# Loads of edge attributes and weights issued by ScalarE; SyncE fetches nine tiles of source rows in place of seven

## The chip, the cores and the metric

The kernel runs on one core of one Trainium2 chip. The metric is the device time of one execution in microseconds (us). A core has TensorE (PE, matmuls; PEld is its weight load), VectorE (DVE), ScalarE (ACT), GpSimd (POOL) and SyncE (SP), each with an instruction queue of its own; they wait for each other through semaphores. SP, ACT and POOL can issue DMAs.

## The reference

A graph layer over N = 6250 nodes of 128 channels and E = 106250 edges, sorted by their destination, followed by a residual sum and a layer norm:

```python
ef  = relu(edge_attr @ We1 + be1) @ We2 + be2          # edge_attr: E x 64
tw  = sigmoid(edge_weight[:, None] @ Wt + bt)          # E x 128
ef  = ef * tw
combined = concatenate([x[src], ef], axis=1)
msg = relu(combined @ Wn1 + bn1) @ Wn2 + bn2
out = segment_sum(msg, dst, N) + x
y   = layernorm(x + out)                               # N x 128
```

All of it is float32.

## The kernel before, in words

**The split of the work.** The first half of `Wn1` meets only `x[src]`, so the kernel first multiplies all nodes, adds `bn1`, and writes the product to DRAM as `node_table` (6250 rows of 512 B). An edge then needs its source's row of that table. `Wn2` is applied after the sum over edges. Edges go in groups of 512, a *pair* is two groups (1024 edges, 8 tiles of 128 edges), a *super* is two pairs (2048 edges). There are 104 pairs and 52 supers.

**One pair, as it runs through the engines.** PE transposes the edge attributes (`psT`, L839), ACT copies them out (`eaT`, L630), PE does the first edge layer (`psH`, L875), ACT its relu (`h<-psH`, L671), PE the second (`psE`, L887), and DVE multiplies it by the edge's weight factor `tw`, an ACT sigmoid (L663), into `efw` (L1162). PE multiplies `efw` by the second half of `Wn1` (`psM`, L862). DVE adds the gathered rows, `h<-psM,gathered` (L1141, function `pre`, semaphore `pre_ready`). ACT does the relu in place (`h<-h`, L596), and PE sums edges over their destinations by a product with one-hot tiles (`psS`, L820), which ACT copies out (`found`, L593) and DVE adds to the sums (L1105). Step s of the program works on all these stages at once, each for a pair further back: `psT`, `psH` and `tw` for pair s, `psE` and `efw` for pair s-1, `psM` and `pre` for pair s-2, `h<-h` and `psS` for pair s-3.

**The order on an engine is the order of the code.** Nothing is scheduled by a tool. Every four steps the loop body repeats (`BODY = 4`), and every four steps some blocks of finished nodes are put out (staging, two small PE products, the layer norm, a store by ACT at L694).

**Gathers.** POOL issues one indirect DMA for each tile of 128 edges (L536), 8 for each pair from pair 4 on, into one of four places of `gathered` (pair modulo 4). Before the gathers of pair p it waits until `pre` of pair p-4 has read that place.

**Rows fetched by SP.** Of some pairs the eighth tile isn't gathered by POOL. SP fetches its 128 rows one by one: it loads 8 node numbers from `src_rows` into registers (L496) and issues one DMA of one row for each (L501), into one of two buffers `row_tiles`; ACT copies the full buffer into `gathered` (`move_rows`, L655, semaphore `rows_moved`), and `pre` of that pair waits for it too. Before, these pairs are 20, 32, 44, ..., 92, so 7 tiles and 896 rows. Tile n+2 may only be fetched when tile n has been moved.

**Loads.** SP also issues the loads of edge attributes (`ea`, L442, 512 KB) and of edge weights (`ew`, L448, 1 MB written, each weight to all 128 partitions), one each for each super, into two buffers. A load of `ea` waits until the transposes of the super two back are done, a load of `ew` until the sigmoids of it are. The rows are paced by these loads: behind a load of `ea` 8 rows, behind a load of `ew` 8 or 16.

Of the kernel before, what the change touches and what calls it, by code (L numbers as in the profile page):

```python
# [40 lines left out]
DVE_ENGINE = mybir.EngineType.DVE  # L41
# [3 lines left out]
P = 128  # L45
TILES = 4
# [22 lines left out]

W1, IDS = W + 1, 13  # L70
ROW_TILE = PAIR * TILES - 1
ROW_LOAD, ROW_EVERY, ROW_FIRST, ROW_FROM = 8, 3, 5, 4


PART = (6, PAIR * TILES - 6)
# [2 lines left out]
def gnn_kernel(nc, x, src, dst, edge_attr, edge_weight, We1, be1, We2, be2, Wt, bt, Wn1, bn1, Wn2, bn2, out):  # L78
# [27 lines left out]
    with ExitStack() as ctx:  # L106
# [168 lines left out]

        def row_pair(n):

            return (ROW_FIRST + n * ROW_EVERY) * BODY

        def row_tile_of(p):  # L280

            turn = p // BODY - ROW_FIRST
            if p % BODY or turn < 0 or turn % ROW_EVERY or p >= PAIRS - 1:
                return None
            return turn // ROW_EVERY

        def row_tiles_by(turn):

            if isinstance(turn, int):
                return max(0, (turn - ROW_FIRST) // ROW_EVERY + 1)  # L290
            return turns["done"]

        def gathered_by(turn):

            if isinstance(turn, int):
                return turn * PART[1] - row_tiles_by(turn)
            return turns["done"] * (ROW_EVERY * PART[1] - 1) + (ROW_FIRST - ROW_EVERY + turns["of"]) * PART[1]

        def wait(eng, semaphore, value):

            if not (isinstance(value, int) and value <= 0):
                eng.wait_ge(semaphore, value)
# [124 lines left out]
        N_WEIGHTS = len(loads_act) + len(loads_sp)  # L427


        @block.sync  # L430
        def _(sp):
            def load_x(c):
                sp.dma_start(x_sb[:, c * XCH:(c + 1) * XCH, :],
                             x_blocks[:, c * XCH:(c + 1) * XCH, :]).then_inc(x_in[c], 16)

            def load_rows(tile, a, landed):
                last, first, second = by_group(a)
                for to, of in ((tile[0:SG, 0, :], last), (tile[SG:P, 0, :], first), (tile[0:ROWS[1], 1, :], second)):
                    sp.dma_start(to, of).then_inc(landed, 16)

            def load_edges(slot, start):
                sp.dma_start(ea[slot][:, :, :],  # L442
                             edge_attr[bass.ds(start, SE), :].rearrange("(g p j) f -> p g (j f)", p=P, j=TILES))\
                    .then_inc(ea_in[slot], 16)

            def load_weights_of(slot, start):

                sp.dma_start(ew[slot][:, :, :].rearrange("p g e -> p (g e)"),  # L448
                             edge_weight[bass.ds(start, SE)].rearrange("(a e) -> a e", a=1).to_broadcast([P, SE]))\
                    .then_inc(ew_in[slot], 16)  # L450

            def load_raw_e(n, a, b):

                part = src[E - SE:E] if a < SG else src[0:SE]
                sp.dma_start(raw_e[:, a:b, :], part.rearrange("(g p j) -> p g j", p=P, j=TILES)
                             [:, a % SG:(b - 1) % SG + 1, :]).then_inc(raw_e_in[n], 16)

            load_raw_e(0, 0, 2)
            for c in range(CHUNKS):
                load_x(c)  # L460
                if c == 1:
                    load_raw_e(1, 2, 4)
                if c == 3:
                    load_raw_e(2, 4, 8)
                    load_rows(src_rows, src, src_in)
            sp.dma_start(x_sb[0:LAST, FULL, 0:C], x_last).then_inc(x_in[CHUNKS], 16)
            load_rows(dst_rows, dst, dst_in)
            for to, of in loads_sp:
                sp.dma_start(to, of).then_inc(weights_in, 16)

            for b, (rows, n) in enumerate(BLOCKS):
                sp.wait_ge(table_ready, b + 1)
                sp.dma_start(table_blocks[:, b, :] if b < FULL else table_last,
                             table_sb[b][0:rows, 0:n * C]).then_inc(table_out[min(b // RING, 2)], 16)
                if b == RING:
                    load_edges(0, E - SE)
            load_weights_of(0, E - SE)
            sp.wait_ge(span_ready, 2)
            for r in range(2):
                sp.dma_start(spans_dram[r * P:r * P + ROWS[r], :], span_i[0:ROWS[r], r, :]).then_inc(span_out, 16)  # L480
            load_edges(1, 0)
            sp.wait_ge(span_out, 32)
            sp.dma_start(spans[:, :, :], spans_dram.rearrange("(a g) k -> a g k", a=1)).then_inc(spans_in, 16)
            for to, of in loads_late:
                sp.dma_start(to, of).then_inc(late_in, 16)
            load_weights_of(1, 0)

            def fetch_rows(n, first, last):

                p = row_pair(n)  # L490
                g = p * PAIR + ROW_TILE // TILES
                j = ORDER[ROW_TILE % TILES]
                if first == 0 and n >= 2:
                    sp.wait_ge(rows_moved, n - 1)
                for at in range(first, last, ROW_LOAD):
                    nodes = nc.values_load_multi_w_load_instructions(  # L496
                        src_rows[g % P:g % P + 1, g // P, at * TILES + j:(at + ROW_LOAD - 1) * TILES + j + 1:TILES],
                        engines=(mybir.EngineType.SP,), min_val=0, max_val=N - 1,
                        skip_runtime_bounds_check_because="an edge's source, which the inputs bound")[1]
                    for r, node in enumerate(nodes):  # L500
                        sp.dma_start(row_tiles[at + r:at + r + 1, n % 2, :], table[bass.ds(node, 1), :])\  # L501
                            .then_inc(rows_in[n % 2], 16)

            sp.wait_ge(src_in, 48)
            wait_table(sp)
            per = 2 * ROW_EVERY
            for m in range(2, SUPERS):
                n, part = (m - ROW_FROM) // per, (m - ROW_FROM) % per
                at = [P * x // ROW_LOAD // per * ROW_LOAD for x in (part, part + 1)]
                fetched = n >= 0 and row_tile_of(row_pair(n)) is not None  # L510
                sp.wait_ge(eaT_ps, (m - 1) * 2)
                load_edges(m % 2, (m - 1) * SE)
                if fetched:
                    fetch_rows(n, at[0], at[0] + ROW_LOAD)
                sp.wait_ge(tw_ready, (m - 1) * 2)
                load_weights_of(m % 2, (m - 1) * SE)
                if fetched:
                    fetch_rows(n, at[0] + ROW_LOAD, at[1])
            sp.wait_ge(last.y_done, 1)
            sp.dma_start(out_last, x_sb[0:LAST, FULL, 0:C]).then_inc(y_out, 16)  # L520

# [40 lines left out]
        def _(act):  # L562
# [48 lines left out]
            def step(i, k):  # L611
# [16 lines left out]
                if live(i, k, 0):  # L628
                    act.wait_ge(eaT_ps, s + 1)
                    nc.scalar.activation(eaT[:, k % 2, :], psT[:, :], ACT.Copy).then_inc(eaT_ready, 1)  # L630
                if s < RAW - RAW_BEFORE - 1:
                    copy_raw(s)
                if s == 0:
# [4 lines left out]
                if live(i, k, 0):  # L638
                    if s < BODY:
                        for n in ([], [0], [1], [2, 3])[s]:  # L640
                            weigh(n)
                    else:
                        weigh(s)
                    if s:
                        relu_h1(s)
                if s == RAW - RAW_BEFORE - 2:
                    copy_raw(s + 1)

# [343 lines left out]
        def _(dve):  # L992
# [174 lines left out]
            def pre(g, i, k):  # L1167
# [3 lines left out]
                if isinstance(g, int) and g < RAW // PAIR:  # L1171
                    rows = raw_pairs[g]
                    if g < RAW_BEFORE // PAIR:
                        dve.wait_ge(table_ready, len(BLOCKS) + (g + 1) * PAIR)
                    else:
                        dve.wait_ge(raw_ready, (g + 1) * PAIR - RAW_BEFORE)
                else:
                    rows = gathered[:, at, :]
                    turn = i - 1 if k < MSG_LAG else i
                    dve.wait_ge(gather_in[place][0], turn * (16 * PART[0]))  # L1180
                    if place == 0:
                        dve.wait_ge(gather_in[place][1], gathered_by(turn) * 16)
                        wait(dve, rows_moved, row_tiles_by(turn))
                    else:
                        dve.wait_ge(gather_in[place][1], turn * (16 * PART[1]))
                make_pre(h[:, at, :], psM[:, :, :], rows).then_inc(pre_ready, 1)
# [260 lines left out]
                    dve.wait_ge(last.shift_ready, 1)  # L1447
                    make_row(last, 0, 0)

            main_loop(dve, DVE_ENGINE, step, finish, end, ahead, ROW_FIRST, ROW_EVERY)  # L1450


# [23 lines left out]
```

## Time and profile before

| | us |
|---|---|
| median of 3 runs | 1438.06 (1436.29 to 1439.51) |
| the profiled execution, its own time | 1437.05 |
| its span in the trace | 1435.3 |
| POOL busy | 783.2 |
| PE busy (PE weight loads) | 966.9 (722.8) |
| DVE busy | 649.6 |
| ACT busy | 580.0 |

No engine is busy all the time, so the busy shares alone don't name a bound: the waits do. "Remote" as the releaser of a wait means that the profile doesn't name who ended it, and the end of a matmul is modelled in the trace. A "q" behind an engine's name marks what its sequencer does, such as the issue of a DMA.

### The profile page before, as it was taken

How to read it: one execution, taken by the hardware profiler on the slowest of the kernel's cores; microseconds unless marked ns; L12 is line 12 of the kernel's file. 1: busy time of each engine (PE TensorE's matmuls, PEld its weight loads, DVE VectorE, ACT ScalarE, POOL GpSimd, SP SyncE). 2: the span in 40 equal slices, each digit the busy share in tenths (PEclk: the TensorE clock that was granted, in tenths of full speed). 3: DMA queues.
4: the chain of work that ended last, by engine and by line, in shares of the span. 5: the costliest groups of instructions: out<-in, count | busy, mean ns of one | idle time of the engine just before them, and what ended most of it. 6: DMA issues, size and time to landing. Idle time of an engine off the chain costs nothing.

```text
span 1435.3 us, 18308 instructions
## 1 busy us (share of the span) xinstructions
PE 966.9 (67%) x5031; PEld 722.8 (50%) x5032; DVE 649.6 (45%) x1688; ACT 580.0 (40%) x656; POOL 783.2 (55%) x834
## 2 busy tenths in 40 slices
PE   3638767676677767666767667676766766765765
PEld 3626544554555545444545455555444545553454
DVE  1425533444445445344444444444543635544446
ACT  1316433443444425443444344443443534442442
POOL 7270456555655555556555565556555555655640
PEclk7768888798898889888878788889988977887978
DMA  6433332333423323333233233333332423333310
GB/s 183 142 110 110 103 114 89 95 114 93 131 83 108 114 88 115 106 100 124 85 91 121 92 101 113 100 121 89 105 114 85 136 86 112 112 102 112 96 30 18
DMA packets 72025, 148.62 MB, mean 104 GB/s; under 512 B 18295, under 2 KB 47030, under 8 KB 65254
## 3 DMA queue, kind: packets, MB, share of 16 engines
q1 hardware_dynamic: 42918, 89.72, 18.4%
q0 software_dynamic: 26400, 54.12, 14.3%
q10 hardware_dynamic: 2592, 3.48, 0.7%
q8 instruction: 45, 0.74, 0.2%
q14 instruction: 70, 0.57, 0.1%
HBM read 140.85 MB, written 6.40 MB: 103 GB/s over the span
## 4 chain that ended last, share of the span: by engine, by line
another core or an unknown queue 42%; ACT 21%; PE 19%; issue 11%; DVE 5%; ACTq 2%; DVEq 0%
ACT tw L663 9%; PE psS L820 6%; PE psM L862 5%; ACT h L596 4%; PE psH L875 4%; PE psE L887 2%; ACT h L671 2%; ACT eaT L630 1%; ACT found L593 1%; ACT x_sb L684 1%; DVE efw L1162 1%; DVE onehot L1147 1%; ACT staged_own L699 1%; DVE h L1141 1%
## 5 line engine op out<-in xcount | busy, mean ns | idle before, releaser
L536 POOL DMA_INDIRECT gathered<-node_table,src_e x793 | 751.6, 948 | 594.6 <-DVE h L1141 328.5
L820 PE MATMUL psS<-onehot,h 128*128 128x128 f32 x1656 | 294.1, 350 | 259.5 <-ACT h L596 234.2
L820 PEld LDWEIGHTS psS<-onehot,h 128*128 128x128 f32 x1656 | 274.2, 258 | 278.3 <-ACT h L596 140.7
L671 ACT ACTIVATE h<-psH,be_c 128x1024 f32<-128x1024 f32 x104 | 115.9, 1115 | 666.4 <-remote 522.0
L1141 DVE TENSOR_TENSOR h<-psM,gathered 128x1024 f32<-128x1024 f32 (+1 forms) x104 | 122.8, 1183 | 552.2 <-remote 503.4
L862 PE MATMUL psM<-wn,efw 128*128 128x128 f32 x1664 | 233.7, 298 | 31.6 <-issue 25.5
L862 PEld LDWEIGHTS psM<-wn,efw 128*128 128x128 f32 x1664 | 226.8, 217 | 29.1 <-issue 21.6
L663 ACT ACTIVATE tw<-ew,bt_c,wt_c 128x1024 f32<-128x1024 f32 x104 | 234.2, 2253 | 4.8 <-DVE efw L1162 3.5
L887 PE MATMUL psE<-h,we 128*128 128x512 f32 x416 | 217.4, 644 | 5.5 <-issue 5.4
L1162 DVE SCALAR_TENSOR_TENSOR efw<-psE,be_c,tw 128x1024 f32<-128x1024 f32 x104 | 133.0, 1279 | 94.4 <-remote 45.3
L1147 DVE TENSOR_SCALAR onehot<-split_ids,dst_e 128x65 f32<-128x65 f32 x832 | 173.8, 271 | 0.3
L887 PEld LDWEIGHTS psE<-h,we 128*128 128x128 f32 x416 | 74.1, 198 | 140.1 <-issue 140.0
L875 PE MATMUL psH<-eaT,we 64*128 64x512 f32 x416 | 128.6, 667 | 16.3 <-issue 15.2
L596 ACT ACTIVATE h<-h 128x1024 f32<-128x1024 f32 (+1 forms) x108 | 110.6, 1026 | 9.4 <-DVE h L1141 9.0
L1155 DVE TENSOR_REDUCE found<-onehot 128x128 f32<-128x512 f32 x104 | 109.9, 1057 | 7.6 <-remote 3.6
L630 ACT ACTIVATE eaT<-psT 128x512 f32<-128x512 f32 x104 | 61.7, 594 | 90.5 <-remote 50.6
L839 PEld LDWEIGHTS psT<-ident,ea 128*128 128x128 f32 x416 | 53.1, 144 | 71.7 <-issue 71.7
L1105 DVE TENSOR_TENSOR acc<-acc,found 128x128 f32 x204 | 58.2, 285 | 40.6 <-ACT found L593 21.2
L839 PE MATMUL psT<-ident,ea 128*128 128x128 f32 x416 | 66.1, 277 | 14.0 <-issue 13.9
L805 PE MATMUL psS<-wn,staged_own 128*128 128x128 f32 x88 | 24.5, 370 | 73.4 <-ACT h L596 41.3
L805 PEld LDWEIGHTS psS<-wn,staged_own 128*128 128x128 f32 x88 | 17.7, 250 | 79.7 <-issue 79.7
L875 PEld LDWEIGHTS psH<-eaT,we 64*128 64x128 f32 x416 | 34.5, 190 | 39.2 <-issue 27.8
(112 smaller groups left out, 363.1 us busy)
## 6 DMA issues: line engine op xcount, KB each, us to landing
ew<-in_edge_weight SPq DMA_DIRECT2D x52, 1024.0 KB
ea<-in_edge_attr SPq DMA_DIRECT2D x52, 512.0 KB
row_tiles<-node_table SPq DMA_DIRECT2D x896, 0.5 KB
gathered<-node_table,src_e POOLq DMA_INDIRECT x793
x_sb<-in_x SPq DMA_DIRECT2D x6, 512.0 KB, 6.3
out_y<-x_sb ACTq DMA_DIRECT2D x12, 256.0 KB
node_table<-gathered SPq DMA_DIRECT2D x7, 256.0 KB, 2.1
node_table<-h SPq DMA_DIRECT2D x4, 256.0 KB
```

The lines of the kernel that those rows point to most:

```text
L536: pool.indirect_dma_start(to, None, rows, bass.IndirectOffsetOnAxis(index, 0)).then_inc(landed, 16)
L596: return nc.scalar.activation(at, at, ACT.Relu)
L663: nc.scalar.activation(tw[:, s % 2, :].rearrange("c (o i m) -> c o i m", o=2, i=2), ew[s // 2 % 2][:, s % 2 * PAIR:(s % 2 + 1) * PAIR, :] ...
L671: nc.scalar.activation(h1[:, s % 2, :], psH[:, :, :].rearrange("p r e -> p (r e)"), ACT.Relu, bias=be1_c[:, :]).then_inc(h1_ready, 1)
L820: return nc.tensor.matmul(to, h[:, (k - SUM_LAG) % BODY * PAIR + q, t * C:(t + 1) * C], hot, start=(t == 0), stop=(t == TILES - 1))
L839: mm = nc.tensor.transpose(psT[:, (a * PAIR + q) * P:(a * PAIR + q + 1) * P], ea[k // 2][:, k % 2 * PAIR + q, a * P:(a + 1) * P], ident[:, :])
L862: mm = nc.tensor.matmul(psM[:, q, t * P:(t + 1) * P], efw[:, (k - MSG_LAG) % 2, of], wn1[:, 1, :], start=True, stop=True)
L875: mm = nc.tensor.matmul(psH[:, a, :], we1[a * F:(a + 1) * F, :], eaT[a * F:(a + 1) * F, k % 2, :], start=True, stop=True)
L887: mm = nc.tensor.matmul(psE[:, r, :], we2[:, :], h1[:, (k - EF_LAG) % 2, r * GE:(r + 1) * GE], start=True, stop=True)
L1141: return nc.vector.tensor_tensor(to, of, rows, ALU.add)
L1147: made = nc.vector.tensor_scalar(onehot[:, (k - MSG_LAG) % 2, q * TILES + t, :].rearrange("p (a b) -> p a b", b=IDS), split_ids[:, :, 0:ID ...
L1162: nc.vector.scalar_tensor_tensor(efw[:, (k - EF_LAG) % 2, :], psE[:, :, :].rearrange("p r e -> p (r e)"), be2_c[:, :], tw[:, (k - EF_LAG) ...
```

## The change

ACT issues the loads of `ea` and `ew` from super 4 on, at odd steps: `ea` right behind the copy `eaT`, `ew` behind the relu of the first layer. SP issues only those of supers 0 to 3, and then the rows of one tile after the other with nothing between them. The row tiles are those of pairs 20, 30, 40, ..., 100, so 9 tiles and 1152 rows. POOL issues 791 gathers of this form in place of 793. Since row tiles now fall on places 0 and 2, `pre` waits for `rows_moved` at both. The counts for the general loop (which a run with wide groups would take) change with it.

```diff
-ROW_LOAD, ROW_EVERY, ROW_FIRST, ROW_FROM = 8, 3, 5, 4
+ROW_LOAD, ROW_EVERY, ROW_FROM = 8, 10, 4
+ROW_PAIR, ROW_TURNS, ROW_TURN = 20, 5, 6
...
         def row_pair(n):
-            return (ROW_FIRST + n * ROW_EVERY) * BODY
+            return ROW_PAIR + n * ROW_EVERY
...
+        def load_edges(eng, slot, start):
+            eng.dma_start(ea[slot][:, :, :],
+                          edge_attr[bass.ds(start, SE), :].rearrange("(g p j) f -> p g (j f)", p=P, j=TILES))\
+                .then_inc(ea_in[slot], 16)
...
-            def fetch_rows(n, first, last):
+            def fetch_rows(n):
...
-                if first == 0 and n >= 2:
-                    sp.wait_ge(rows_moved, n - 1)
-                for at in range(first, last, ROW_LOAD):
+                wait(sp, rows_moved, n - 1)
+                for at in range(0, P, ROW_LOAD):
...
+            for m in range(2, ROW_FROM):
+                sp.wait_ge(eaT_ps, (m - 1) * 2)
+                load_edges(sp, m % 2, (m - 1) * SE)
+                sp.wait_ge(tw_ready, (m - 1) * 2)
+                load_weights_of(sp, m % 2, (m - 1) * SE)
             sp.wait_ge(src_in, 48)
             wait_table(sp)
-            per = 2 * ROW_EVERY
-            for m in range(2, SUPERS):
-                n, part = (m - ROW_FROM) // per, (m - ROW_FROM) % per
-                at = [P * x // ROW_LOAD // per * ROW_LOAD for x in (part, part + 1)]
-                fetched = n >= 0 and row_tile_of(row_pair(n)) is not None
-                sp.wait_ge(eaT_ps, (m - 1) * 2)
-                load_edges(m % 2, (m - 1) * SE)
-                if fetched:
-                    fetch_rows(n, at[0], at[0] + ROW_LOAD)
-                sp.wait_ge(tw_ready, (m - 1) * 2)
-                load_weights_of(m % 2, (m - 1) * SE)
-                if fetched:
-                    fetch_rows(n, at[0] + ROW_LOAD, at[1])
+            for n in range(PAIRS // ROW_EVERY):
+                if row_tile_of(row_pair(n)) is not None:
+                    fetch_rows(n)
...
                     nc.scalar.activation(eaT[:, k % 2, :], psT[:, :], ACT.Copy).then_inc(eaT_ready, 1)
+                    m = s // 2 + 2
+                    if k % 2 == 1 and ROW_FROM <= m < SUPERS:
+                        load_edges(act, m % 2, (m - 1) * SE)
...
                         relu_h1(s)
+                        if k % 2 == 1 and ROW_FROM <= m < SUPERS:
+                            act.wait_ge(tw_ready, s + 1)
+                            load_weights_of(act, m % 2, (m - 1) * SE)
...
-                    if place == 0:
-                        dve.wait_ge(gather_in[place][1], gathered_by(turn) * 16)
-                        wait(dve, rows_moved, row_tiles_by(turn))
+                    if place % 2 == 0:
+                        dve.wait_ge(gather_in[place][1], gathered_by(turn, place) * 16)
+                        wait(dve, rows_moved, row_tiles_by(turn, place))
```

On ACT, in one odd step, there stands before (each row is an instruction; the names are those of the code, and in brackets is what it waits for):

```order
L593 ACTIVATE found<-psS 128x2x64 [waits sum_ps]
L596 ACTIVATE h<-h 128x1024 [waits pre_ready]
L630 ACTIVATE eaT<-psT 128x512 [waits eaT_ps]
L663 ACTIVATE tw<-ew,bt_c,wt_c 128x1024 [waits efw_ready]
L671 ACTIVATE h<-psH,be_c 128x1024 [waits h1_ps]
```

and now, in the same step:

```order
L590 ACTIVATE found<-psS 128x2x64 [waits sum_ps]
L593 ACTIVATE h<-h 128x1024 [waits pre_ready]
L627 ACTIVATE eaT<-psT 128x512 [waits eaT_ps]
L434 DMA ea<-in_edge_attr 128x4x256
L666 ACTIVATE tw<-ew,bt_c,wt_c 128x1024 [waits efw_ready]
L674 ACTIVATE h<-psH,be_c 128x1024 [waits h1_ps]
L440 DMA ew<-in_edge_weight 128x2048 [waits tw_ready]
```

The two DMA rows are new, one ahead of the sigmoid and one behind the relu of the first layer, and so ahead of the next step's `found` and `h<-h`.

On SP, where the rows begin, there stands before (a load of node numbers, then a register move and a DMA for each row):

```order
L448 DMA ew<-in_edge_weight 128x2048 [waits tw_ready]
L442 DMA ea<-in_edge_attr 128x4x256 [waits eaT_ps]
L496 TENSOR_LOAD src_rows
L501 ISA
L501 DMA row_tiles<-node_table 1x128
```

and now:

```order
L440 DMA ew<-in_edge_weight 128x2048 [waits tw_ready]
L498 TENSOR_LOAD src_rows [waits table_out1,table_out2,table_out0,src_in]
L503 ISA
L503 DMA row_tiles<-node_table 1x128
L503 ISA
```

The load of `ea` for super 4, with its wait, no longer stands ahead of the first row, and none of the later loads stands between rows.

## Rows read from the trace of the kernel before

**Rows 1.** The page: span, and busy time of the engines.

```profile
span 1435.3 us, 18308 instructions
PE 966.9 (67%) x5031; PEld 722.8 (50%) x5032; DVE 649.6 (45%) x1688; ACT 580.0 (40%) x656; POOL 783.2 (55%) x834
```

**Rows 2.** The waits, whole span: who waited for whom, us in total, times, longest.

```profile
ACT h L671 <- remote: 522.0, 68, 12.3
DVE h L1141 <- remote: 519.3, 80, 15.9
POOL gathered L536 <- DVE h L1141: 328.5, 77, 41.6
PE psS L820 <- ACT h L596: 234.2, 58, 8.5
...
ACT tw L663 <- DVE efw L1162: 3.5, 11, 0.4
```

**Rows 3.** The timeline from 604 us on, POOL, DVE, ACT and PE.

```profile
604.55 0.94 POOL L536 DMA_INDIRECT gathered<-node_table,src_e  x1 [3.69 <-DVE h L1141]
605.80 0.94 POOL L536 DMA_INDIRECT gathered<-node_table,src_e  x1 [0.30 <-issue]
...
613.30 0.95 POOL L536 DMA_INDIRECT gathered<-node_table,src_e  x1 [0.30 <-issue]
608.22 1.95 PE L862 MATMUL psM<-wn,efw 128*128 128x128 f32 x16
615.01 1.23 DVE L1141 TENSOR_TENSOR h<-psM,gathered 128x1024 f32<-128x1024 f32 x1 [7.03 <-remote]
615.75 1.11 ACT L671 ACTIVATE h<-psH,be_c 128x1024 f32<-128x1024 f32 x1 [7.99 <-remote]
616.76 0.27 ACT L593 ACTIVATE found<-psS 128x128 f32<-128x128 f32 x1
617.19 1.07 ACT L596 ACTIVATE h<-h 128x1024 f32<-128x1024 f32 x1
618.31 3.78 PE L820 MATMUL psS<-onehot,h 128*128 128x128 f32 x16 [4.73 <-ACT h L596]
617.01 0.95 POOL L536 DMA_INDIRECT gathered<-node_table,src_e  x1 [2.76 <-DVE h L1141]
```

**Rows 4.** POOL and DVE behind them; pair 44 has a row tile.

```profile
624.51 0.94 POOL L536 DMA_INDIRECT gathered<-node_table,src_e  x1 [0.30 <-issue]
627.04 1.22 DVE L1141 TENSOR_TENSOR h<-psM,gathered 128x1024 f32<-128x1024 f32 x1 [6.61 <-remote]
640.43 1.23 DVE L1141 TENSOR_TENSOR h<-psM,gathered 128x1024 f32<-128x1024 f32 x1 [6.36 <-remote]
653.73 1.23 DVE L1141 TENSOR_TENSOR h<-psM,gathered 128x1024 f32<-128x1024 f32 x1 [3.95 <-remote]
```

**Rows 5.** DVE around 1245 us; pair 92 has a row tile.

```profile
1239.54 1.23 DVE L1141 TENSOR_TENSOR h<-psM,gathered 128x1024 f32<-128x1024 f32 x1 [6.45 <-remote]
1245.78 1.23 DVE L1141 TENSOR_TENSOR h<-psM,gathered 128x1024 f32<-128x1024 f32 x1 [0.83 <-PE psM L862]
1262.68 1.23 DVE L1141 TENSOR_TENSOR h<-psM,gathered 128x1024 f32<-128x1024 f32 x1 [9.64 <-remote]
```

**Rows 6.** SP's timeline; then by source line: ns min/median/max, first and last start in us.

```profile
124.20 0.33 SPq L448 DMA_DIRECT2D ew<-in_edge_weight  x1
...
L501 SPq DMA_DIRECT2D row_tiles<-node_table x896: 2/228/1383, 137.6 to 1212.7; - x180
L448 SPq DMA_DIRECT2D ew<-in_edge_weight x52: 3/338/704, 64.4 to 1344.8; - x52
L442 SPq DMA_DIRECT2D ea<-in_edge_attr x52: 11/412/700, 50.7 to 1340.0; - x52
L655 ACT ACTIVATE gathered<-row_tiles x7: 309/309/310, 318.2 to 1248.0; 128x128 f32<-128x128 f32 x7
```

**Rows 7.** SP's own waits from 137 to 1213 us.

```profile
SPq L442 <- PE psT L839: 102.0, 17, 12.5
SPq L442 <- remote: 58.9, 10, 18.8
```

**Rows 8.** ACT's timeline around a store of a block of nodes.

```profile
654.80 1.64 ACT L684 ACTIVATE x_sb<-staged_own,shift,rstd 128x128 f32 x4
656.61 0.35 ACTq L694 DMA_DIRECT2D out_y<-x_sb  x1
657.07 0.28 ACT L593 ACTIVATE found<-psS 128x128 f32<-128x128 f32 x1 [0.63 <-ACT x_sb L684]
```

**Rows 9.** Windows of L1141: length, DVE busy (x instructions), clock, DMA.

```profile
221.00:1199.00 978.00, 91.84 (x75) 0.84 0.34 105
1199.00:1389.00 190.00, 18.37 (x15) 0.83 0.31 95
```

More of the change, by code:

```diff
@@ L276, in row_pair, with row_tiles_by, gathered_by @@
         def row_pair(n):
-            return (ROW_FIRST + n * ROW_EVERY) * BODY
+            return ROW_PAIR + n * ROW_EVERY
         def row_tile_of(p):
[L282 to L287, printed above, removed]
-            if isinstance(turn, int):
-                return max(0, (turn - ROW_FIRST) // ROW_EVERY + 1)
-            return turns["done"]
-        def gathered_by(turn):
+            after = p - ROW_PAIR
+            return after // ROW_EVERY if after >= 0 and after % ROW_EVERY == 0 and p < PAIRS - 1 else None
+        def row_tiles_by(turn, place, of_place=False):
+            if isinstance(turn, int):
+                fetched = [p for p in range(turn * BODY + place + 1) if row_tile_of(p) is not None]
+                return len([p for p in fetched if p % BODY == place] if of_place else fetched)
+            first = ROW_TURN - ROW_TURNS + turns["of"]
+            return row_tiles_by(first, place, of_place) + turns["done"] * (1 if of_place else ROW_TURNS * BODY // ROW_EVERY)
+        def gathered_by(turn, place):
             if isinstance(turn, int):
-                return turn * PART[1] - row_tiles_by(turn)
-            return turns["done"] * (ROW_EVERY * PART[1] - 1) + (ROW_FIRST - ROW_EVERY + turns["of"]) * PART[1]
+                return turn * PART[1] - row_tiles_by(turn, place, True)
+            first = ROW_TURN - ROW_TURNS + turns["of"]
+            return (turns["done"] * (ROW_TURNS * PART[1] - 1)
+                    + (first * PART[1] - row_tiles_by(first, place, True)))
         def wait(eng, semaphore, value):
@@ L427, in gnn_kernel, with load_weights_of @@
         N_WEIGHTS = len(loads_act) + len(loads_sp)
+        def load_edges(eng, slot, start):
+            eng.dma_start(ea[slot][:, :, :],
+                          edge_attr[bass.ds(start, SE), :].rearrange("(g p j) f -> p g (j f)", p=P, j=TILES))\
+                .then_inc(ea_in[slot], 16)
+        def load_weights_of(eng, slot, start):
+            eng.dma_start(ew[slot][:, :, :].rearrange("p g e -> p (g e)"),
+                          edge_weight[bass.ds(start, SE)].rearrange("(a e) -> a e", a=1).to_broadcast([P, SE]))\
+                .then_inc(ew_in[slot], 16)
         @block.sync
@@ L439, in load_rows @@
                     sp.dma_start(to, of).then_inc(landed, 16)
[L441 to L450, printed above, removed]
             def load_raw_e(n, a, b):
@@ L475, in _ @@
                 if b == RING:
-                    load_edges(0, E - SE)
-            load_weights_of(0, E - SE)
+                    load_edges(sp, 0, E - SE)
+            load_weights_of(sp, 0, E - SE)
             sp.wait_ge(span_ready, 2)
@@ L480, in _ @@
                 sp.dma_start(spans_dram[r * P:r * P + ROWS[r], :], span_i[0:ROWS[r], r, :]).then_inc(span_out, 16)
-            load_edges(1, 0)
+            load_edges(sp, 1, 0)
             sp.wait_ge(span_out, 32)
@@ L485, in _ @@
                 sp.dma_start(to, of).then_inc(late_in, 16)
-            load_weights_of(1, 0)
-            def fetch_rows(n, first, last):
+            load_weights_of(sp, 1, 0)
+            def fetch_rows(n):
                 p = row_pair(n)
@@ L1448, in end @@
                     make_row(last, 0, 0)
-            main_loop(dve, DVE_ENGINE, step, finish, end, ahead, ROW_FIRST, ROW_EVERY)
+            main_loop(dve, DVE_ENGINE, step, finish, end, ahead, ROW_TURN, ROW_TURNS)
 _INS = ['x', 'src', 'dst', 'edge_attr_64', 'edge_weight', 'L0_gnn_We1', 'L0_gnn_be1', 'L0_gnn_We2', 'L0_gnn_be2',
```

## The prediction

> **What bounds the kernel now.** I read the page, then the waits, then the timeline of a few pairs, then one line at a time. The page [rows 1] names no engine that is full: PE is busy 67% of the span, POOL 55%. The waits [rows 2] close in a ring. POOL waits 328.5 us for DVE's addition (`pre`, L1141), DVE's addition waits 519.3 us and ACT's first-layer relu 522.0 us for something that the profile doesn't name, and PE waits 234.2 us for ACT's relu behind `pre`.
>
> The timeline [rows 3] shows what one turn of the ring is. POOL issues its eight gathers from 604.55 us at a pitch of 1.25 us (604.55, 605.80), the last starts at 613.30 and ends at 614.25. The matmuls that `pre` waits for are recorded until 610.17 us, yet `pre` starts at 615.01, 0.76 us behind the end of POOL's last gather, and those gathers are for a pair three further on, which `pre` doesn't need. ACT's relu of PE's next product comes right behind, at 615.75. POOL starts again at 617.01, 0.77 us behind the end of `pre`. In the next pairs it is alike: the gathers that end at 625.45 are followed by `pre` at 627.04 [rows 4], 1.59 us later. So while POOL issues gathers, what PE has finished seems to become visible late; it comes through when POOL is done. I don't know the mechanism; the trace shows only that the two go together. A turn is then eight gathers (9.7 us), the release (0.8 to 1.8), `pre` (1.23) and POOL's restart (0.77), some 13.4 us, as between 627.04, 640.43 and 653.73 (13.39 and 13.30) [rows 4]. Over long stretches the pace is 978/75 = 13.04 us a pair [rows 9], since now and then PE gets through early: 6.24 us from 1239.54 to 1245.78, with 16.90 behind it [rows 5].
>
> PE comes close behind: its products end a few us ahead of the release in some turns and with it in others. The loads of weights are not waited for: ACT's sigmoid, their reader, waits 3.5 us in the whole span, and that for DVE [rows 2].
>
> **The change part by part.**
>
> *Two gathers fewer.* The pair with a row tile has seven gathers. In rows 4 the batch of pair 44 starts at 617.01 and its last gather starts at 624.51, and `pre` follows `pre` by 12.03 us (615.01 to 627.04) in place of 13.39 and 13.30 behind it: 1.3 us less, one pitch of 1.25. That is the nearest price, as it is the plain one. At pair 92 [rows 5] the short batch let PE through early, and two turns took 1262.68 - 1239.54 = 23.14 us in place of 2 x 13.4 = 26.8: 3.7 us less. From below, a shorter batch brings nothing where PE is the later one: 0. I take 1.25 for each of the two added tiles: **-2.5 us**; bounds 0 and -7.4.
>
> *The tiles moved.* The old ones stood in pairs 20, 32, 44 and so on, all at place 0; four of the new nine (30, 50, 70, 90) stand at place 2, behind other small work of PE and ACT. That can take the 3.7 from some and leave 1.25. It is inside the bounds above: at worst all seven old tiles brought 3.7 and all nine new 1.25, which would be +14.6, a value that pair 44 itself speaks against. 0.
>
> *ACT issues 96 loads* (48 of `ea`, 48 of `ew`). SP needs 0.41 us (median) for one of `ea` and 0.34 for one of `ew`, up to 0.70 [rows 6]; ACT needs 0.35 for a store [rows 8]. Where they stand: `ea` behind the start of the copy `eaT`, and ahead of the sigmoid, which waits for nothing urgent and whose reader is one step later. `ew` stands behind the relu of the first layer (1.11 us [rows 3]) and ahead of `found` and `h<-h`, which PE waits for. If ACT's sequencer issues while the relu still runs, 0.35 to 0.70 lie under 1.11 us: 0. Rows 3 show `found` starting 1.01 us behind the relu's start, so the next instruction is already there when the relu ends. If the issue stands between the two, each costs its own length: the store in rows 8 leaves ACT idle for 0.63 us, though that one also waits for the block's last row. Bounds 0 and 48 x 0.70 = +34 for `ew`; for `ea` the same 34 at most, under POOL's batch. I take **0**: ACT idles 522 us in all before that relu [rows 2], and a turn doesn't end before POOL's batch does. If the cover is gone, PE's sums start 0.35 us later in every other turn.
>
> *SP's loads go away, 256 rows come.* From 137 to 1213 us SP waited 102.0 + 58.9 = 161 us [rows 7], so it worked 1076 - 161 = 915 us for 896 rows [rows 6] and about 84 loads at 0.4 (34 us): (915 - 34)/896 = 0.98 us a row, 126 us a tile. Supply: the moves of tiles stand at 318.2 and 1248.0 [rows 6], six gaps of 12 pairs, 12.91 us a pair; a tile every 10 pairs has 129 us. The fetch can now start behind the issue of the weights of super 3, at 124.2 us [rows 6]. Tile 0 is then ready at 250 and needed at 318; tile 8 is needed at 318 + 80 x 12.91 = 1351, and at 0.98 ready by 124 + 1152 x 0.98 = 1253. No row is late as long as one takes less than (1351 - 124)/1152 = **1.065 us**. I take 0; what SP does is else on nobody's path.
>
> Here a rule of the Trainium skill speaks against the change: DMA: Bandwidth & Descriptors, "Issuing engines are not separate DMA queues", says that starting DMAs from several engines saves only the sequencer's time, which is usually small. By it the move frees 34 us of SP's time, room for 35 rows and not for 256, and the ninth tile would be late. Rows 7 show the larger part: the 161 us that SP stood waiting between its rows, which goes too. A run must show whether a row costs the same with nothing between.
>
> *Two more moves and waits.* Two copies of 0.31 us on ACT [rows 6], under POOL's batch or 0.6 at most; the added waits of DVE at place 2 are for tiles moved two steps earlier: 0. Nothing queued behind them is new.
>
> Sum: -2.5. The profiled execution took 1437.05, so 1434.6; the median of the runs shown is 1.0 higher, so **1435.6** in its terms, 0.17% less. This measurement can tell about 0.2% (2.9 us) from no change, so the forecast is at the edge of that.
>
> **The rivals.**
>
> *A. More turns get through early.* With SP's loads gone, or with tiles more often, PE's release comes early in more turns. Such an event is worth 2.4 us by rows 5 (the 3.7 less the gather's 1.25); four more of them make -9.8, with the gathers -12.3: 1426. For: the early ones come unevenly, so something small decides them. Against: nothing says that the change pushes that way. Chance 0.14.
>
> *B. ACT's issues stand on the path.* If the issue of `ew` waits for the relu to end, 48 x 0.35 = +17, less 2.5: 1452; with half of it hidden behind POOL's batch 1444. For: `found` and `h<-h` are what PE waits for. Against: ACT's idle time. It decides from 0.11 us for each pair of loads on (5.4 us in all). Chance 0.20.
>
> *C. Rows come late.* SP's row time rises, since it now also works in the stretches in which it used to wait, which are those of POOL's batches. At 1.08 us the last tile is 17 us late, at 1.10 it is 124 + 1267 = 1391, 40 us late, and ACT stands at `move_rows` for it with `h<-h` behind: 1453 to 1475. It decides at 1.065, 8% above what I count. Chance 0.10.
>
> *D. Rows cost the others time.* Behind the last row a pair takes 190/15 = 12.67 us, with rows 13.04 [rows 9]; with six and one row tiles counted back at 1.25, 13.14 and 12.75. If the 0.39 us belong to the 12 rows of a pair, 256 more rows cost +8, less 2.5: 1444. Fifteen pairs are few, and two early turns more explain it as well. Chance 0.10.
>
> The main case has 0.46, with a range of its own of 1430.7 to 1438.1.
>
> **How the numbers follow.** The main case puts 0.22 below 1435.2 and the rest within 0.2%, with a little above. With A, faster is 0.36. B and D give 0.06 to no change, so same is 0.30, and slower 0.34. The range leaves out the lower half of A and, above, C and the upper part of B: 1427 to 1451.
>
> **What would show it.** In the changed trace: seven-gather batches nine times, with the turn behind them 1.3 us or more shorter; `pre` still 0.8 to 1.8 us behind POOL's last gather; ACT's `found` still about 1.0 us behind the relu's start in steps with an `ew` load (if it is 1.4 or more, B); each L655 move without a wait for rows, and rows at under 1.065 us each (else C); the number of turns under 12 us (A). It is wrong if the release doesn't follow POOL's batch any more, for then the gathers are no term at all.

## The result, and the profile after

The changed kernel took 1448.38 us (median of 4 runs, 1447.48 to 1459.1) beside 1437.17 of the kernel before in the same comparison: a ratio of 1.0092, 95% interval 1.0058 to 1.0127, slower by 13 us by that ratio, where 0.17% less was forecast. A second comparison on another chip gave 1.0081 (1.0050 to 1.0112). The profiled execution took 1448.68 us, its span 1446.9.

The page of the changed kernel has hardly changed in its busy times, against [rows 1]:

```profile
span 1446.9 us, 19131 instructions
PE 980.8 (68%) x5031; PEld 742.9 (51%) x5032; DVE 647.7 (45%) x1688; ACT 579.4 (40%) x658; POOL 780.5 (54%) x832
q10 hardware_dynamic: 34848, 78.98, 15.7%
q1 hardware_dynamic: 11174, 14.35, 3.3%
```

The loads of the loop have gone to ACT's queue (q10); on SP's (q1) are left the rows and what is loaded and stored ahead of the loop and behind it. The waits, in the columns of [rows 2], are the same ring with more time in it:

```profile
ACT h L674 <- remote: 576.8, 72, 11.0
DVE h L1144 <- remote: 539.9, 81, 20.1
POOL gathered L533 <- DVE h L1144: 354.0, 82, 41.3
PE psS L823 <- ACT h L593: 278.6, 70, 7.8
```

ACT waits 55 us longer ahead of its first-layer relu, POOL 26 us longer for DVE, PE 44 us longer for ACT. Which part of the change did it? The timeline of ACT in one odd step, to hold against [rows 3], answers for the loads:

```profile
635.65 1.11 ACT L674 ACTIVATE h<-psH,be_c 128x1024 f32<-128x1024 f32 x1 [8.25 <-remote]
635.66 0.34 ACTq L440 DMA_DIRECT2D ew<-in_edge_weight  x1
636.66 0.27 ACT L590 ACTIVATE found<-psS 128x128 f32<-128x128 f32 x1
636.85 1.06 ACT L593 ACTIVATE h<-h 128x1024 f32<-128x1024 f32 x1
```

The issue of `ew` takes 0.34 us from 635.66 on, beside the relu, and `found` starts 1.01 us behind the relu's start, as before. So in this step the loads cost ACT nothing. The rows by source line, and SP's own wait between 124 and 1228 us, answer for lateness; the columns are those of [rows 6] and [rows 7]:

```profile
L503 SPq DMA_DIRECT2D row_tiles<-node_table x1152: 2/225/783, 126.1 to 1227.1; - x192
L658 ACT ACTIVATE gathered<-row_tiles x9: 309/309/320, 317.7 to 1361.1; 128x128 f32<-128x128 f32 x9
SPq L498 <- ACT gathered L658: 17.9, 4, 7.6
```

SP fetched 1152 rows in 1101 us less 17.9 of waiting: 0.94 us a row. The last row is issued at 1227, and ACT moves the last tile at 1361. SP even waited for buffers to come free. Nobody waits for a row.

What did change is how often a turn of the ring is short. Windows over DVE's addition (length, DVE busy and count, clock, DMA), with rows being fetched and behind the last row:

```profile
304.40:1226.70 922.30, 85.70 (x70) 0.83 0.32 103
1226.70:1399.70 173.00, 17.14 (x14) 0.84 0.30 99
```

While SP fetches, a pair takes 922.3/70 = 13.18 us; behind the last row 173/14 = 12.36. In [rows 9] the two were 13.04 and 12.67. I also counted turns, as the distances of the starts of L1144 from pair 7 to pair 101 (94 turns): 63 lie between 13 and 14 us and 10 under 11, where before 51 and 16 did. A turn between 13 and 14 has the length of one that waits for POOL's batch of eight. How an early one looks, behind the last row, and a held one, in the middle (DVE's timeline):

```profile
1352.62 1.23 DVE L1144 TENSOR_TENSOR h<-psM,gathered 128x1024 f32<-128x1024 f32 x1 [5.06 <-remote]
1358.87 1.23 DVE L1144 TENSOR_TENSOR h<-psM,gathered 128x1024 f32<-128x1024 f32 x1 [0.83 <-PE psM L865]
1375.85 1.22 DVE L1144 TENSOR_TENSOR h<-psM,gathered 128x1024 f32<-128x1024 f32 x1 [9.73 <-remote]
```

```profile
622.23 1.22 DVE L1144 TENSOR_TENSOR h<-psM,gathered 128x1024 f32<-128x1024 f32 x1 [7.85 <-remote]
635.59 1.23 DVE L1144 TENSOR_TENSOR h<-psM,gathered 128x1024 f32<-128x1024 f32 x1 [7.95 <-remote]
649.11 1.23 DVE L1144 TENSOR_TENSOR h<-psM,gathered 128x1024 f32<-128x1024 f32 x1 [6.49 <-remote]
```

### The profile page after: what moved, and what is told of

The parts are those of the page before. It is cut to its first block, busy times and chain, and to the rows that moved or that the text cites. A ratio compares the mean times of both kernels' runs of the same rounds, so it can differ in the third digit from the quotient of the medians.

```text
span 1446.9 us, 19131 instructions
## 1 busy us (share of the span) xinstructions
PE 980.8 (68%) x5031; PEld 742.9 (51%) x5032; DVE 647.7 (45%) x1688; ACT 579.4 (40%) x658; POOL 780.5 (54%) x832
## 4 chain that ended last, share of the span: by engine, by line
another core or an unknown queue 45%; ACT 23%; PE 17%; issue 9%; DVE 3%; ACTq 2%; DVEq 0%
ACT tw L666 11%; PE psS L823 6%; ACT h L593 5%; PE psM L865 4%; PE psH L878 3%; ACT eaT L627 2%; ACT h L674 2%; ACT found L590 1%; PE psE L890 1%; ACT staged_own L702 1%; ACT x_sb L687 1%; DVE efw L1165 1%; PE psS L808 1%; PE psS L809 1%
## 5 line engine op out<-in xcount | busy, mean ns | idle before, releaser
L823 PE MATMUL psS<-onehot,h 128*128 128x128 f32 x1656 | 311.6, 365 | 292.5 <-ACT h L593 278.6
L823 PEld LDWEIGHTS psS<-onehot,h 128*128 128x128 f32 x1656 | 290.8, 272 | 312.3 <-ACT h L593 174.9
L1144 DVE TENSOR_TENSOR h<-psM,gathered 128x1024 f32<-128x1024 f32 (+1 forms) x104 | 122.8, 1183 | 582.5 <-remote 519.8
L865 PE MATMUL psM<-wn,efw 128*128 128x128 f32 x1664 | 240.5, 305 | 18.2 <-issue 12.6
L865 PEld LDWEIGHTS psM<-wn,efw 128*128 128x128 f32 x1664 | 234.8, 224 | 18.4 <-issue 11.9
L878 PE MATMUL psH<-eaT,we 64*128 64x512 f32 x416 | 123.9, 659 | 6.6 <-issue 5.4
```

What stands on the lines that cost most here:

```text
L823: return nc.tensor.matmul(to, h[:, (k - SUM_LAG) % BODY * PAIR + q, t * C:(t + 1) * C], hot, start=(t == 0), stop=(t == TILES - 1))
L865: mm = nc.tensor.matmul(psM[:, q, t * P:(t + 1) * P], efw[:, (k - MSG_LAG) % 2, of], wn1[:, 1, :], start=True, stop=True)
L878: mm = nc.tensor.matmul(psH[:, a, :], we1[a * F:(a + 1) * F, :], eaT[a * F:(a + 1) * F, k % 2, :], start=True, stop=True)
L1144: return nc.vector.tensor_tensor(to, of, rows, ALU.add)
```

## The experiments

The chips differ: the kernel before has its median between 1437 and 1456 us on them. So all comparisons are ratios to the kernel before on the same chip, and 0.1% is 1.4 us.

**Loads and rows apart.** Four kernels, of which two fetch no row and two fetch seven tiles. `p1_no_rows` is the kernel before with this, and with the counts that follow from it:

```diff
         def row_tile_of(p):
-            turn = p // BODY - ROW_FIRST
-            if p % BODY or turn < 0 or turn % ROW_EVERY or p >= PAIRS - 1:
-                return None
-            return turn // ROW_EVERY
+            return None
```

> The kernel before, with no row tile at all: SyncE fetches no rows, GpSimd gathers all 800 tiles of this form (7 more), loads stay on SyncE. Nothing else changes. Theory R (each row that SyncE fetches while the loop runs holds back the early turns of TensorE, so rows cost more than the gather they save): in the changed kernel the stretch behind the last row runs at 12.36 us a pair and the stretch with rows at 13.17, so without rows all 100 pairs should run near 12.6 to 12.9, and the time is 10 to 30 us under that of before (1407 to 1427) in spite of seven gathers more. Theory L (rows are harmless, and what cost the changed kernel its time is that the loads come from ScalarE at another moment): seven gathers more cost 7 x 1.25 = +9 us, near 1446.

`p2_act_loads_no_rows` is the changed kernel with the same edit to its own `row_tile_of`.

> The changed kernel (loads from ScalarE) with no row tile at all, GpSimd gathers all 800 tiles. Beside the kernel before without rows it differs in the loads alone. Theory R: the same time as that kernel, within 3 us, and 20 to 40 us under the changed kernel (1448). Theory L: 10 us or more above the kernel before without rows, since the loads from ScalarE are the cost.

`p3_act_loads_seven` is the changed kernel with the tiles of before:

```diff
-ROW_LOAD, ROW_EVERY, ROW_FROM = 8, 10, 4
-ROW_PAIR, ROW_TURNS, ROW_TURN = 20, 5, 6
+ROW_LOAD, ROW_EVERY, ROW_FROM = 8, 12, 4
+ROW_PAIR, ROW_TURNS, ROW_TURN = 20, 3, 5
```

> The changed kernel with the seven row tiles of before (pairs 20, 32, ..., 92), fetched without pacing. Theory R: 256 rows fewer than in the changed kernel, with 0.03 to 0.06 us a row, take off 8 to 15 us, and two gathers come back at +2.5: 1436 to 1443. Theory L: only the two gathers count, so 1448 + 2.5, near 1450.

`p4_act_loads_paced` adds SP's waits of before between its rows:

```diff
+            for m in range(ROW_FROM, SUPERS):
...
+                sp.wait_ge(eaT_ps, (m - 1) * 2)
+                if fetched:
+                    fetch_rows(n, at[0], at[0] + ROW_LOAD)
+                sp.wait_ge(tw_ready, (m - 1) * 2)
+                if fetched:
+                    fetch_rows(n, at[0] + ROW_LOAD, at[1])
```

> As the run with seven row tiles and loads from ScalarE, but SyncE waits between its rows for the same two semaphores as in the kernel before, so the rows stand at the moments of before; beside the kernel before only the loads are moved to ScalarE. Theory R: the time of before within 4 us (1433 to 1441). Theory L: near the changed kernel, 1446 to 1451. A third view, P (it is the pacing that matters, rows bunched against pairs): this one as before, and the unpaced one with seven tiles 5 us or more above it.

Measured, as ratios with their 95% intervals:

| | no rows | 7 tiles, paced | 7 tiles, unpaced | 9 tiles, unpaced |
|---|---|---|---|---|
| loads on SP | 0.9820 (0.9784 to 0.9857) | 1 (before) | | |
| loads on ACT | 0.9785 (0.9752 to 0.9817) | 0.9980 (0.9955 to 1.0004) | 1.0026 (1.0003 to 1.0048) | 1.0092 (1.0058 to 1.0127), another chip |

Theory R, rows hold the others back, is what the table shows: without any row the kernel is 1.8% faster, though POOL has seven gathers more. Theory L falls: with the same rows behind the same waits, loads from ACT are 0.20% below loads from SP, which the interval doesn't tell from nothing. Without rows they are 0.35% (5 us) below, where at most 3 us were expected; the two intervals overlap. The pacing makes 0.46%. The two tiles more make 0.66% across chips (0.55% by the second comparison).

The table also gives a price for a row, on one chip (1454 us before), with the seven gathers that the rows save counted back at 1.3 us each: (26 + 9)/896 = 0.039 us with loads on SP, and (35 + 9)/896 = 0.049 us unpaced with loads on ACT.

**The fetching alone.** All four start from the kernel with loads on ACT and no row tile; SP does something that nobody uses. `q1_rows_unused` fetches as the changed kernel does, and waits only for its own buffers:

```diff
-            for n in range(PAIRS // ROW_EVERY):
-                if row_tile_of(row_pair(n)) is not None:
-                    fetch_rows(n)
+            for n in range(9):
+                if n >= 2:
+                    sp.wait_ge(rows_in[n % 2], n // 2 * (16 * P))
+                fetch_rows(n)
```

> Loads from ScalarE, GpSimd gathers all 800 tiles, and SyncE fetches 1152 rows as in the changed kernel, but nobody reads them and nobody waits for them but SyncE itself (once for each buffer and at the end). Against the run without rows (0.9785 of before) it holds the pure cost of the fetching. Theory R: the rows cost 25 to 40 us, so it stands at 0.996 to 1.006 of before plus 11 us for the nine gathers that the changed kernel saves: 1.003 to 1.014. If rows cost only through ScalarE's wait for them and its copies, it is at 0.98.

`q2_dma_only` has in place of `fetch_rows(n)`:

```diff
+                for r in range(P):
+                    at = (n * P + r) * 5
+                    sp.dma_start(row_tiles[r:r + 1, n % 2, :], table[at:at + 1, :]).then_inc(rows_in[n % 2], 16)
```

> As the run with unused rows, but the addresses are constants: the same 1152 one-row DMAs on SyncE with no load of node numbers and no register moves (other rows of the table are read). Theory R-dma (the issue or the landing of each small DMA is what disturbs): the same cost as with node numbers, 25 to 40 us above the run without rows. Theory R-load (the register loads from SBUF disturb): within 5 us of the run without rows, 0.975 to 0.983 of before.

`q3_loads_few_dma` keeps the loads of node numbers, with `for r, node in enumerate(nodes[:1])`.

> As the run with unused rows, but of each eight rows only one is fetched: the same 144 loads of eight node numbers, 144 DMAs in place of 1152. Theory R-dma: an eighth of the cost, 3 to 5 us above the run without rows (0.981 of before). Theory R-load: the full cost, 25 to 40 us (1.00).

`q4_wide_dma` is `q2_dma_only` with steps of 8 rows, `row_tiles[r:r + 8, ...]` and `table[at:at + 8, :]`.

> As the run with constant addresses, but eight neighbouring rows in one DMA: 144 DMAs of 4 KB in place of 1152 of 512 B, the same bytes into the same buffers. If the number of DMAs is what costs: 3 to 5 us above the run without rows. If the bytes or the traffic into SBUF cost: as much as with 1152.

The run without rows stands at 0.9785, 0.9843 and 0.9810 of before in three comparisons, 0.9813 in the mean. None of them was on the chip of these four, so each difference below is uncertain by some 4 us either way. Against it:

| run | ratio to before (95%) | DMAs | above 0.9813 |
|---|---|---|---|
| q1_rows_unused | 1.0206 (1.0180 to 1.0231) | 1152, with node numbers | 56 us, 0.049 each |
| q2_dma_only | 1.0001 (0.9982 to 1.0020) | 1152, constant addresses | 27 us, 0.023 each |
| q3_loads_few_dma | 0.9893 (0.9869 to 0.9917) | 144, with 144 loads of 8 numbers | 11 us |
| q4_wide_dma | 0.9847 (0.9817 to 0.9877) | 144 of 4 KB | 5 us, inside the spread |

So it is the number of SP's small DMAs, and more so with addresses from registers; the same bytes in 144 DMAs cost little. Two of the four missed what was expected: `q1_rows_unused` stands at 1.0206, above the 1.003 to 1.014, and `q3_loads_few_dma` costs 11 us and not 3 to 5, so loading the node numbers may have a part of its own; it stands 0.0046 above `q4_wide_dma`, and the intervals overlap a little. `q1_rows_unused` is the changed kernel plus nine gathers, less ACT's moves, and stands 0.0114 above it across chips (16 us, against 9 x 1.25 = 11 by the pitch).

Where the DMAs stop, the loop gets faster. Here are the windows of DVE's addition in `q2_dma_only`, whose last DMA is issued at 518.3 us, then in `q1_rows_unused`, whose last is at 1211.1, and then in `p2_act_loads_no_rows`, which has none. Each window begins and ends with the start of an addition:

```profile
172.70:528.80 356.10, 31.83 (x26) 0.84 0.32 100
528.80:1405.00 876.20, 84.51 (x69) 0.84 0.34 103
```

```profile
173.20:1218.30 1045.10, 95.50 (x78) 0.82 0.32 101
1218.30:1432.40 214.10, 20.81 (x17) 0.82 0.31 94
```

```profile
169.40:501.20 331.80, 31.84 (x26) 0.83 0.34 105
501.20:1383.50 882.30, 84.49 (x69) 0.82 0.33 103
```

That is 13.70 and 12.70 us a pair in the first, 13.40 and 12.59 in the second, and 12.76 and 12.79 where no row is fetched. In `q2_dma_only` the excess of 1.00 us over 26 pairs makes 26 us, nearly all of the 27: the cost lies in the stretch in which the DMAs are issued, within one trace. The clock is the same in both of its stretches, 0.84. The counts of turns point the same way: between 13 and 14 us are 31 of 94 without rows, 43 with constant addresses, 62 with node numbers; under 11 us 28, 21 and 11.

**The gather's price.** The disputed term by itself, 99 pairs at once. `q5_seven_gathers` is the kernel with loads on ACT and without rows, and leaves out the gather of one tile of each pair, so that its sums are of other rows:

```diff
-PART = (6, PAIR * TILES - 6)
+PART = (5, 2)
...
-                        if row_tile_of(p) is not None and q * TILES + t == ROW_TILE:
+                        if p < PAIRS - 1 and q * TILES + t == 3:
                             continue
```

> The kernel without rows, with seven gathers of each pair in place of eight: the fourth tile of each pair keeps what its buffer held, so its sums are of other rows; all else is as it was. It measures the term of the prediction, what one gather less is worth, over 99 pairs at once. Theory G (a turn of the ring is POOL's gathers and then the release): 99 x 1.25 = 124 us less than without rows, 0.89 of before. Theory T (TensorE and its chain are the later one in most turns, and the release only looks as if it followed POOL): less than 60 us, above 0.94.

`q6_six_gathers` leaves out two, with `in (2, 3)` and `PART = (4, 2)`.

> As with seven gathers, with six in each pair (the third and fourth tile keep what their buffers held). Theory G: another 124 us less, 0.81 of before, until TensorE's own work (some 9.3 us a pair busy) is met. Theory T: about the same time as with seven.

Beside them ran the changed kernel and the best version again:

> The changed kernel once more, beside the two kernels that it is to be compared with. Theory R (SyncE's small DMAs hold back TensorE's early turns): 1.006 to 1.013 of before, as at first; 1.03 of the kernel without rows.

> The best version so far, loads from ScalarE and no row fetched by SyncE, once more on the same chip as the changed kernel: 0.976 to 0.983 of before, and under both kernels in every run.

| run | ratio to before (95%) |
|---|---|
| after_again | 1.0081 (1.0050 to 1.0112) |
| act_loads_no_rows_again | 0.9843 (0.9812 to 0.9875) |
| q5_seven_gathers | 0.8945 (0.8916 to 0.8974) |
| q6_six_gathers | 0.8092 (0.8067 to 0.8116) |

The changed kernel is 1.024 of the one without rows here, where 1.03 was expected. With its nine gathers counted back at 1.3 us its rows cost (35 + 12)/1152 = 0.040 us each.

Before has 1452 us here, so the first gather taken from each pair is worth 0.0898 x 1452/99 = 1.32 us and the second 0.0853 x 1452/99 = 1.25. Theory G holds in full, though PE was busy 69% of the span in the run with eight. The windows of DVE's addition with eight, seven and six gathers, one kernel each, all on this chip:

```profile
160.00:1390.00 1230.00, 116.27 (x95) 0.82 0.34 103
```

```profile
160.00:1270.00 1110.00, 116.32 (x95) 0.86 0.35 108
```

```profile
160.00:1150.00 990.00, 116.35 (x95) 0.91 0.36 114
```

12.9, 11.7 and 10.4 us a pair. The granted clock rises with it, 0.82, 0.86 and 0.91, while PE is busy 69, 74 and 76% of the span. How much of the gain is the clock's no run separates; both steps lie close to the pitch of 1.25.

**Which property of a small DMA.** Left open so far was whether the moment in a turn or the small size of a one-row DMA makes the cost. `q7_sixteen_rows` issues 1152 DMAs of 16 rows each. They aren't back to back, since SP waits until eight have landed before it issues the next eight:

```diff
+                for r in range(P):
...
+                    to = r % 8 * 16
+                    if r >= 8 and r % 8 == 0:
+                        sp.wait_ge(rows_in[n % 2], n // 2 * (16 * P) + 16 * r)
+                    sp.dma_start(row_tiles[to:to + 16, n % 2, :], table[at:at + 16, :]).then_inc(rows_in[n % 2], 16)
```

`q8_at_release` and `q9_mid_batch` issue twelve one-row DMAs for each of 96 pairs behind a wait:

```diff
+            for i in range(96 * 12):
+                s, n, r = i // 12 + 5, i // P, i % P
+                if i % 12 == 0:
+                    sp.wait_ge(msg_ps, s)          # q9_mid_batch: sp.wait_ge(tw_ready, s + 3)
...
+                at = i * 5
+                sp.dma_start(row_tiles[r:r + 1, n % 2, :], table[at:at + 1, :]).then_inc(rows_in[n % 2], 16)
```

> The anchor: loads from ScalarE, no rows. 0.978 to 0.986 of before.

> 1152 DMAs with constant addresses back to back, each of 16 neighbouring rows (8 KB) into 16 partitions, so that it spreads over DMA engines; sixteen times the bytes, the same number. If the number of issues is what costs: the 27 us of one-row DMAs, 0.019 above the anchor. If a DMA on one engine is what costs: under 8 us. If bytes cost: more than 27 us.

> 1152 one-row DMAs with constant addresses, twelve for each of 96 pairs, issued when TensorE's product for the pair is released (in GpSimd's pause between two batches of gathers). If it costs where it falls into the turn: under 10 us above the anchor here, and 40 us or more in the other. If each DMA costs by itself: 27 us, 0.019 above the anchor, in both.

> The same twelve DMAs for each pair, issued when ScalarE's sigmoid of a later pair is done, some 3 us into GpSimd's batch of gathers. If it costs where it falls into the turn: 40 us or more above the anchor (0.028). If each DMA costs by itself: 27 us, as in the other.

The anchor is the kernel with loads on ACT and without rows, run beside the three:

| run | ratio to before (95%) | above the anchor |
|---|---|---|
| act_loads_no_rows_c | 0.9810 (0.9784 to 0.9836) | |
| q7_sixteen_rows | 0.9978 (0.9958 to 0.9997) | 24 us, 0.021 a DMA |
| q8_at_release | 1.0033 (1.0013 to 1.0054) | 32 us, 0.028 |
| q9_mid_batch | 0.9970 (0.9950 to 0.9990) | 23 us, 0.020 |

My guess that it costs where it falls into POOL's batch is wrong, since the order of the two is the other way round, 32 at the release and 23 in the batch, with intervals that just don't meet. The two aren't a clean contrast: twelve DMAs take over 3 us to issue, and by their starts in the traces 52% of those of `q8_at_release` still fall between the first and the last gather of a batch, and 79% of those of `q9_mid_batch`. Sixteen times the bytes cost no more, at a slower pace (936 - 123 = 813 us for 1152 DMAs, 0.71 us each, beside 0.34 in `q2_dma_only`):

```profile
L519 SPq DMA_DIRECT2D row_tiles<-node_table x1152: 3/420/1911, 123.1 to 936.3; - x192
```

So with a constant address a DMA costs some 0.02 to 0.03 us in all four ways of issuing it. Whether it is the issue, the transfer or the count of its semaphore no run separates, since every DMA here has all three.

## Why the prediction was wrong, point by point

**The ring** was right. Turns are bound by POOL's batch and the release behind it, and a gather less is worth one pitch: 1.25 forecast, 1.32 and 1.25 measured over 99 pairs of the kernels without rows. The term of -2.5 us stands.

**ACT's issues at 0** was right, and rival B fell: 0.34 us under the relu, `found` at 1.01 us, and the ratio of loads on ACT to loads on SP with the same rows 0.9980.

**No row late** was right, and rival C fell: 0.94 us a row where 0.98 was counted and 1.065 would have been too much. From the rule on issuing engines (DMA: Bandwidth & Descriptors of the Trainium skill, "Issuing engines are not separate DMA queues") the prediction had worked out, as an objection, that the time freed on SP would not carry the ninth tile; it did, since SP's waits went too. The rule's own claim, that only sequencer time is saved, agrees with 0.9980.

**The step that failed** is "I take 0; what SP does is else on nobody's path". It is on no path that the waits name, and still the rows cost: 56 us for 1152 of them in `q1_rows_unused`, 0.049 us each, and 0.040 each in the changed kernel beside the one without rows. The 256 rows more then cost +10 to +12.5 us, and the two gathers less give back 2.6: +8 to +10, where the change from seven tiles to nine measured +0.66% (9.5 us) and +0.55% (8 us). The rest is the pacing, +0.46% (6.6 us): the forecast counted the waits that go from between SP's rows as time for more rows, and put no price on rows that come without them. The loads take off 2.9 us. That the three steps add up to 13 us is no check, since the ratio of the last one was taken from the result itself; what is checked is that the price of a row, from other runs, gives the step from seven to nine.

**Rival D** had the mechanism, from the stretch behind the last row [rows 9], at +8 for 256 rows in place of +10 to +12.5, and I gave it 0.10, on the ground that 15 pairs are few. They were few indeed. Stretches of 70 and 14 pairs in `p2_act_loads_no_rows`, which fetches no row, differ by nearly as much:

```profile
298.70:1199.80 901.10, 85.72 (x70) 0.83 0.34 105
1199.80:1375.60 175.80, 17.14 (x14) 0.82 0.32 98
```

That is 12.87 and 12.56 us a pair, and in `p1_no_rows` 12.85 and 13.08. So the 0.37 us of [rows 9] lie little outside what fourteen pairs vary by, and that they came near the price of a row is in part luck. But the alternative, that what SP does can't matter as nobody waits for it, had no row in its favour at all.

**Rival A** went the other way: with the loads gone from SP and more rows fetched there were fewer early turns, 10 and not 16.

**What stays open.** Why PE's finished products are seen late while POOL issues gathers, why rows with addresses from registers cost up to twice those with constants (in the counts they take away more early turns), and why unpaced rows cost more than paced ones. Also where in the turn the cost sits. Early turns alone don't carry it: `q8_at_release` costs 32 us and has 21 turns under 11 us, where its anchor without rows, `act_loads_no_rows_c`, has 25. Between 13 and 14 us it has 42 where the anchor has 30; twelve such turns at 13.48 in place of 12.61, the mean of the anchor's others, make 10 us, and the rest lies in longer turns of the other kinds.

## What to carry to other kernels

A transfer that nobody waits for isn't free: price the issue of many small DMAs by comparing the loop's pace with and without them. A stretch of each in the same trace can point to it, but fourteen pairs are too few to size it, since the kernels without rows differ by up to 0.3 us a pair between fourteen pairs near their end and the seventy ahead of them; a run without the DMAs sizes it. Work moved from the engine that bounds the loop to an idle queue must be counted there in issues, not in bytes: here a gather of 128 rows is worth 1.3 us on POOL and cost 5 to 6 us as single rows on SP (128 x 0.040 to 0.049). The version to keep is the one with loads from ACT and no row tiles at all, 0.979 to 0.984 of before in three comparisons and faster than both kernels; with loads on SP it is 0.982, so the edit that pays is to leave the rows out.

## What the runs showed of the hardware

One-row DMAs issued by SP slow this loop, which doesn't wait for them, by 0.02 to 0.03 us each with constant addresses and 0.04 to 0.05 with addresses from registers, and a DMA of 16 rows costs no more than one of a single row (0.021 us). And a TensorE that is busy 69% of the span can still be the one that waits: leaving out an eighth of POOL's gathers took 9% of the time before off the time, and another eighth nearly as much again, while PE's granted clock went from 0.82 to 0.91.
